# Attention and mixture-of-experts on one Trainium2 core: where the row transposes of the expert blocks stand, and a new placement of the attention part's steps

## What is computed

```python
x = x + retention(layernorm(x), ctx, ctx)       # 16 heads, decayed causal scores, no softmax
x = x + linear_fp8(layernorm(x), kernel, bias)  # input and weights rounded to float8_e4m3fn
x = x + attention(layernorm(x), ctx)            # softmax over 512 context tokens, 16 heads of 16
x = x + experts(layernorm(x))                   # 8 experts of width 512, 4 chosen per token

# experts, for each token n and each of its 4 experts e:
gate, up = split(x[n] @ gate_up[e].T + bias[e]) # 512 each
act = (clip(up, -7, 7) + 1) * min(gate, 7) * sigmoid(1.702 * gate)
y[n] += share[n, e] * (act @ down[e].T + down_bias[e])
```

## Time and profile before

| | |
|---|---|
| runs shown, median (lowest to highest of 3) | 1029.71 us (1019.78 to 1035.69) |
| the profiled execution | 1026.56 us |
| its span, first to last instruction | 1024.8 us |
| mean granted TensorE clock over the span | 0.887 of full speed |
| busy: TensorE, VectorE, ScalarE, GpSimd | 814.2, 641.1, 488.8, 281.7 us |
| first part, about | 0 to 615 us |
| listing the tokens, first blocks | 615 to 666 us |
| blocks 2 to 38 and the last scatters | 666 to 1025 us |

### The profile page before, as it was taken

The page is one execution under the profiler, slowest core; times in us unless marked ns, Lnnn a source line. Parts: engine busy times, 40 slices in busy tenths (PEclk is TensorE's granted clock), DMA queues, the critical chain, the costliest instruction groups (busy, mean ns, idle before and its releaser), DMA issues. The chain is left out here.

```text
span 1024.8 us, 18540 instructions
## 1 busy us (share of the span) xinstructions
PE 814.2 (79%) x6353; PEld 508.4 (50%) x6353; DVE 641.1 (63%) x1238; ACT 488.8 (48%) x950; POOL 281.7 (27%) x261
## 2 busy tenths in 40 slices
PE   0682676778858898887877988999899998999893
PEld 0342232333424343422322354778787887878782
DVE  4546566876687779677788328455555555555552
ACT  1210301455424654366577521466666666666662
POOL 5004003010211000000000002265556555655543
PEclk9895777679868999898696997899999999999997
DMA  7421461016111531034434113133333333333332
GB/s 270 123 60 64 132 167 43 32 54 159 66 50 47 159 75 48 23 106 159 139 125 155 33 41 104 34 55 58 59 64 59 56 57 64 61 56 60 59 43 31
DMA packets 72072, 83.22 MB, mean 81 GB/s; under 512 B 10288, under 2 KB 65200, under 8 KB 71856
## 3 DMA queue, kind: packets, MB, share of 16 engines
q1 hardware_dynamic: 57008, 61.25, 19.5%
q0 software_dynamic: 14976, 20.78, 12.7%
HBM read 52.71 MB, written 29.29 MB: 80 GB/s over the span
## 5 line engine op out<-in xcount | busy, mean ns | idle before, releaser
L1600 PE MATMUL gu_ps<-xt,w 128*128 128x256 f16 x1872 | 215.8, 276 | 29.1 <-ACT xt L1321 29.1
L1600 PEld LDWEIGHTS gu_ps<-xt,w 128*128 (+1 forms) x1872 | 181.7, 99 | 62.9 <-issue 39.5
L672 ACT ACTIVATE p<-st 128x512 f32<-128x512 f32 x256 | 138.7, 595 | 125.2 <-PE st L1156 124.8
L883 DVE TENSOR_REDUCE neg_max<-sc 128x2 f32<-128x1024 f32 x128 | 156.3, 1221 | 59.7 <-PE sc L1132 58.9
L1391 POOL DMA_INDIRECT out<-y,block_rows x78 | 125.1, 1604 | 139.7 <-ACT y L1351 118.6
L1614 PE MATMUL dn_ps<-w,h 128*128 (+1 forms) x936 | 108.6, 273 | 1.4 <-DVE h L1518 1.4
L1509 DVE TENSOR_SCALAR up<-up 128x512 f32<-128x512 f32 x78 | 42.6, 546 | 96.8 <-ACT up L1337 96.8
L1383 POOL DMA_INDIRECT gx<-xr_d,block_rows x78 | 86.0, 1102 | 53.1 <-DVE block_rows L1491 30.1
L1132 PE MATMUL sc<-kz,sq 48*128 48x512 f16 x256 | 63.2, 462 | 42.4 <-DVE neg_max L883 38.7
L1614 PEld LDWEIGHTS dn_ps<-w,h 128*128 128x128 f16 x936 | 89.9, 98 | 11.4 <-issue 1.6
L580 POOL COPY rden_rows<-rden 128x512 f32<-128x512 f32 x16 | 10.8, 677 | 266.8 <-DVE rden L904 266.8
(11 more groups left out here) (200 smaller groups left out, 1114.4 us busy)
## 6 DMA issues: line engine op xcount, KB each, us to landing
stack_d<-t SPq DMA_DIRECT2D x16, 256.0 KB, 2.6
raw<-in_gate_up_t SPq DMA_DIRECT2D x4, 1024.0 KB, 5.0
raw_next<-in_gate_up_t SPq DMA_DIRECT2D x4, 1024.0 KB, 5.6
sq<-stack_d SPq DMA_DIRECT2D x16, 192.0 KB, 3.6
kz<-stack_d SPq DMA_DIRECT2D x16, 192.0 KB, 4.6
sq<-stack_d SPq DMA_DIRECT2D x32, 96.0 KB, 3.2
kz<-stack_d SPq DMA_DIRECT2D x32, 96.0 KB, 3.2
ctx_pad<-in_ctx SPq DMA_DIRECT2D x4, 512.0 KB, 4.0
```

Of the source, the lines that this page charges most:

```text
L672: act.activation(p32[:, n // 2 % RING, 2 * (n % 2) + i, :], st[:, i, :], ACT.Exp, scale=QSCALE).then_inc(s_exp, 1)
L883: dve.tensor_reduce(neg_max[:, qt, :, pair], sc[:], AX.X, ALU.max, negate=True).then_inc(m_max, 1)
L1600: ins = pe.matmul(gu_ps[:, 2 * half + g, q * ROWS:(q + 1) * ROWS], weights(i, wi, slice(col, col + P)), xt[:, i % 2, kd, xi, :], start=(j ...
```

## The change

It has two parts that don't touch each other. In the second part, TensorE issues `turn_x(i+2)` between the two halves of `gate_up(i+1)` instead of behind both; ScalarE issues `take_x(i+2)` ahead of the first `high_half` of block i+1 instead of behind its second `unit`; VectorE issues `collect(i)` ahead of the last `low_half` of block i+1 instead of behind it. In the first part every entry of `ORDER` is new. The steps, their number and what each issues stay, but for the fillers, whose number depends on the order.

```diff
             for i in range(NB):                       # ScalarE
                 if i + 1 < NB:
                     unit(2 * i + 2)
+                    if i + 2 < NB:
+                        take_x(i + 2)
                     high_half(2 * i + 2)
                     unit(2 * i + 3)
-                    if i + 2 < NB:
-                        take_x(i + 2)
                     high_half(2 * i + 3)
                 scale_y(i)
...
                     low_half(2 * i + 2)               # VectorE
                     take_share(i + 1)
                     unit(2 * i + 3)
+                collect(i)
+                if i + 1 < NB:
                     low_half(2 * i + 3)
-                collect(i)
...
-            def gate_up(i):                           # TensorE
+            def gate_up(i, half):
                 pe.wait_ge(xt_ok, i + 1)
-                for half in range(2):
-                    n = 2 * i + half
+                n = 2 * i + half
...
             for i in range(NB):
                 if i + 1 < NB:
                     look_up(i + 1)
-                    gate_up(i + 1)
+                    gate_up(i + 1, 0)
                 if i + 2 < NB:
                     turn_x(i + 2)
+                if i + 1 < NB:
+                    gate_up(i + 1, 1)
                 down(i)
```

Of `ORDER`, the entries that matter below (one tuple per batch):

```diff
-     "quantise": ((84, 89, 93), (250, 256, 263), (504, 505, 506), (777, 785, 793)),
+     "quantise": ((83, 85, 93), (217, 235, 250), (514, 523, 531), (833, 835, 842)),
-     "turn_q": ((97, 99), (271, 287), (511, 516), (812, 827)),
+     "turn_q": ((96, 100), (263, 268), (551, 566), (848, 862)),
-     "max_turn": ((205, 251, 326, 393), (503, 558, 644, 745), (808, 870, 929, 989), (1052, 1112, 1173, 1240)),
+     "max_turn": ((206, 267, 323, 394), (485, 559, 626, 716), (800, 868, 927, 990), (1051, 1109, 1186, 1242)),
-     "turn4": ((739, 746), (950, 965), (1252, 1254), (1313, 1314)),
+     "turn4": ((660, 727), (937, 985), (1168, 1180), (1313, 1314)),
-     "route": ((757,), (974,), (1262,), (1317,)),
+     "route": ((732,), (993,), (1193,), (1317,)),
-     "qk_store": ((39, 41, 128, 150), (175, 177, 353, 388), (489, 493, 646, 675), (805, 809, 925, 967)),
+     "qk_store": ((37, 41, 128, 150), (174, 176, 346, 360), (495, 497, 669, 684), (817, 818, 953, 974)),
```

More of the change, by code:

```diff
@@ L1588, in turn_x @@
                 ins.then_inc(x_tr, 1)
-            def gate_up(i):
+            def gate_up(i, half):
                 pe.wait_ge(xt_ok, i + 1)
-                for half in range(2):
-                    n = 2 * i + half
[L1594 to L1603, removed]
+                n = 2 * i + half
+                for g, (mm, ok) in enumerate(((gate_mm, glu_ok), (up_mm, up_ok))):
+                    need(pe, ok, n - 1)
+                    for q in range(2):
+                        for kd in range(KD):
+                            col = kd * 2 * I + g * I + (2 * half + q) * P
+                            for j, (wi, xi) in enumerate(WX):
+                                ins = pe.matmul(gu_ps[:, 2 * half + g, q * ROWS:(q + 1) * ROWS], weights(i, wi, slice(col, col + P)),
+                                                xt[:, i % 2, kd, xi, :], start=(j == 0 and kd == 0),
+                                                stop=(j == 2 and kd == KD - 1))
+                    ins.then_inc(mm, 1)
             def down(i):
@@ L1653, in _ @@
             list_expert(3)
-            gate_up(0)
+            gate_up(0, 0)
+            gate_up(0, 1)
             for e in range(4, E):
@@ L1682 @@
[L1682 to L1695, removed]
@@ L1709 @@
[L1709 to L1715, removed]
@@ L1763 @@
-     "max_turn": ((205, 251, 326, 393), (503, 558, 644, 745), (808, 870, 929, 989), (1052, 1112, 1173, 1240)),
-     "score": ((218, 222, 226, 236, 241, 253, 257, 261, 276, 283, 289, 296, 304, 311, 316, 319, 361, 372, 380, 387,
[6 rows of a table removed]
-     "values": ((237, 242, 258, 264, 298, 306, 317, 327, 381, 395, 405, 433, 443, 474, 475, 486), (549, 569, 590, 605,
-        634, 640, 658, 688, 703, 751, 753, 761, 774, 782, 790, 799), (851, 863, 883, 898, 912, 937, 943, 956, 984,
-        991, 1003, 1014, 1028, 1040, 1054, 1065), (1099, 1106, 1120, 1139, 1154, 1167, 1182, 1194, 1214, 1227, 1242,
-        1251, 1276, 1286, 1291, 1296)),
@@ L1775 @@
[L1775 to L1779 removed]
+     "turn0_store": ((10, 16, 28, 32), (94, 99, 132, 144), (232, 249, 350, 377), (541, 561, 636, 658)),
@@ new lines @@
+     "stack0": ((36, 52), (142, 168), (369, 412), (653, 740)),
+     "qk_store": ((37, 41, 128, 150), (174, 176, 346, 360), (495, 497, 669, 684), (817, 818, 953, 974)),
+     "next_ctx": ((76,), (200,), (462,)),
+     "stack1": ((138, 147, 159, 165), (363, 381, 428, 487), (707, 713, 719, 801), (967, 979, 1005, 1054)),
+     "next_ctx_t": ((39,), (153,), (507,)),
+     "next_x": ((116,), (309,), (590,), (901,)),
+     "max_store": ((210, 271, 336, 397), (493, 565, 640, 722), (810, 872, 931, 995), (1061, 1114, 1191, 1248)),
@@ new lines @@
+     "x_back": ((124,), (698,), (959,), (1214,)),
+     "out_store": ((662,), (939,), (1166,), (1312,)),
+     "w_load": ((1011, 1013, 1079, 1087, 1125, 1157, 1226, 1253),),
+     "share_store": ((765,), (1031,), (1215,)),
+     "rotate_k": ((3,), (84,), (215,), (489,)),
+     "root": ((1, 81, 113), (115, 209, 303), (312, 502, 593), (599, 809, 908)),
+     "den_spread": ((279, 375, 443, 506), (585, 682, 758, 821), (881, 966, 1023, 1070), (1163, 1218, 1272, 1300)),
+     "root_a": ((632,), (917,), (1135,), (1308,)),
@@ new lines @@
+     "turn0_high": ((7, 14, 24, 27), (89, 95, 130, 137), (229, 238, 347, 364), (516, 552, 627, 642)),
+     "normalise": ((2, 82, 114), (118, 213, 307), (315, 505, 598), (604, 812, 911)),
+     "state_low": ((11, 25), (91, 107), (262, 330), (550, 573)),
+     "qk_high": ((33, 38, 126, 135), (141, 160, 333, 352), (367, 388, 655, 673), (709, 723, 947, 960)),
+     "r_take": ((50, 57, 71, 77), (167, 178, 192, 201), (411, 425, 445, 467), (726, 743, 777, 792)),
+     "v_take": ((18, 22), (55, 59), (499, 508), (814, 822)),
@@ new lines @@
+     "linear_scale": ((105, 109), (276, 287), (575, 588), (878, 894)),
+     "turn3_take": ((120, 122), (318, 324), (633, 645), (921, 926)),
+     "exp": ((220, 222, 225, 239, 242, 248, 254, 257, 290, 295, 301, 308, 319, 328, 334, 341, 355, 372, 380, 391, 402,
[6 rows of a table added]
+     "o_take": ((264, 362, 437, 494), (556, 664, 748, 807), (874, 955, 1014, 1065), (1149, 1211, 1268, 1297)),
+     "normalise_a": ((648,), (918,), (1144,), (1309,)),
+     "rows_high": ((652,), (929,), (1154,), (1310,)),
+     "turn4_take": ((671, 730), (942, 988), (1174, 1184), (1315, 1316)),
@@ new lines @@
+     "w_high": ((1050, 1058, 1062, 1073, 1076, 1078, 1095, 1101, 1108, 1126, 1132, 1139, 1164, 1167, 1176, 1194, 1202,
+        1208, 1252, 1258, 1262, 1277, 1278, 1284),),
+     "route_exp": ((751,), (1019,), (1206,)),
+     "stats": ((0, 80, 111), (112, 207, 297), (305, 484, 591), (592, 804, 903)),
+     "turn0_low": ((8, 15, 26, 30), (90, 97, 131, 140), (230, 244, 348, 366), (536, 558, 631, 646)),
+     "state_sum": ((9, 20), (88, 104), (258, 322), (543, 570)),
+     "rotate": ((4,), (121,), (327,), (606,)),
@@ new lines @@
+     "o_norm": ((288, 393, 454, 586), (612, 691, 763, 828), (886, 981, 1034, 1080), (1185, 1229, 1281, 1302)),
+     "x_bias": ((134,), (721,), (989,), (1250,)),
+     "o_add": ((603, 618), (857, 871), (1093, 1099), (1305, 1306)),
+     "stats_a": ((625,), (909,), (1128,), (1307,)),
+     "rows_low": ((656,), (933,), (1162,), (1311,)),
+     "route_take": ((738,), (1001,), (1199,), (1318,)),
+     "w_low": ((1056, 1063, 1074, 1084, 1085, 1086, 1107, 1113, 1120, 1137, 1145, 1151, 1171, 1190, 1223, 1235, 1241,
+        1247, 1257, 1261, 1266, 1279, 1283, 1288),),
@@ new lines @@
+     "choose": ((739,), (1007,), (1201,)),
+     "weigh": ((761,), (1028,), (1209,)),
+     "turn0": ((6, 12, 21, 23), (87, 92, 125, 133), (226, 233, 338, 351), (510, 547, 622, 637)),
+     "state": ((5, 17), (86, 101), (227, 316), (504, 563)),
+     "r_scores": ((42, 44, 46, 49, 60, 64, 67, 70), (155, 157, 161, 166, 184, 186, 188, 191), (398, 403, 407, 410,
+        424, 432, 438, 444), (680, 686, 692, 725, 762, 769, 773, 776)),
+     "qk": ((29, 34, 123, 129), (139, 149, 329, 345), (361, 385, 649, 670), (685, 718, 930, 954)),
@@ new lines @@
+     "r_outs": ((47, 54, 68, 74), (163, 172, 189, 196), (408, 416, 441, 459), (720, 736, 774, 783)),
+     "r_back": ((58, 61, 73, 78), (170, 180, 194, 203), (414, 430, 448, 471), (729, 745, 781, 796)),
+     "v": ((13, 19), (51, 56), (491, 501), (806, 815)),
+     "turn_q": ((96, 100), (263, 268), (551, 566), (848, 862)),
+     "linear": ((103, 108), (273, 284), (574, 584), (875, 891)),
+     "turn3": ((117, 119), (310, 320), (629, 641), (915, 922)),
+     "maxima": ((145, 148, 152, 171, 177, 181, 195, 199, 211, 214, 218, 231, 236, 245, 251, 259, 272, 277, 283, 289,
[6 rows of a table added]
@@ new lines @@
```

(6 more changed lines are left out.)

63 lines of the change are left out of this document (14 added, 49 removed), and 48 rows, old and new, of the table ORDER.

## The result

The changed kernel takes 990.93 us (median of 4 runs, 983.78 to 991.85); the kernel before, beside it, 1029.24 us (4 runs). The ratio is 0.9642, with a 95% interval of 0.9557 to 0.9727: faster, by 38 us. The forecast was 982, with a range of 968 to 1003. The sign, the range and the expert part came true; the first part didn't give what the sum took for it, and one reason given for the expert part was not the cause, as the experiments show.

What follows compares the result with a forecast made beforehand. The prediction took a ScalarE and VectorE dependency loop to bound the expert blocks. Expert part -37.3 and first part -10.3 took the profiled 1026.56 us to 979.0, forecast as a 982 us median, range 968 to 1003.

Steps and rivals of the forecast that it cites:

- The ring: Expert blocks: a dependency loop through ScalarE and VectorE, `glu` to `glu`, sets 9.13 us a block and shrinks to 8.15.
- Rival 1: Expert blocks: ScalarE and VectorE stay the bound at 8.4 or 8.5 us a block, total 989 us; chance 0.16.
- rival 3: Expert blocks: transposes in mid-block wait themselves, some 9.1 us a block, total 1014 us; chance 0.04.
- The 0.92 that goes: Expert blocks: TensorE's 0.92 us idle before each block's gate matmuls goes, as moved transposes ready `xt` some 3 us early.
- 8.25 us a block: Expert blocks: TensorE becomes the bound at 8.25 us, from 9.247 on average, saving 35.9 us over 36 blocks.
- The first two blocks and the end: Expert part's edges: first two blocks, at low clock, gain about nothing; the last `y_raw` comes 1.4 us earlier.
- TensorE's table loads: Expert blocks: loads of 0.54 to 1.48 us hide behind the previous `down`, cost 0; without cover, 6 us.
- The fillers: First part's tail: filler matmuls fall from 113 to 84, taking 6.3 us off the path.
- The rest of the order: First part, steps in new places: -4 us for one long wait, 0 for everything else, ends +15 and -8.
- 8.27-us wait: First part: TensorE's idle before 294.25 during batch 1's quantising on VectorE; between -8.3 and 0 us, taken as -4.
- rival 2: First part: the new order brings 0 to +9 us while the expert part gives -37.3, total 992 to 1001; chance 0.20.
- rival 4: First part: more idle lowers TensorE's mean clock; from about 0.73 it eats the whole gain, at 0.70 1043 us; chance 0.04.

Runs made afterwards that it cites:

- e9: Kernel before with only VectorE's `collect` moved ahead of the last `low_half`, transposes left behind both halves: 991.93 us, ratio 0.9646.
- e4: Kernel before, old order, with transposes between the halves and `take_x` early, but `collect` left behind the last `low_half`: 1030.62 us, one run.
- e3: Kernel before with the three expert-block edits, old order, no fillers ahead of `turn4` of batches 0 to 2: 983.92 us, ratio 0.9568.
- e7: Same kernel as e3, run again on another chip (expert-block edits, old order, `turn4` fillers only for the last batch): 986.24 us, ratio 0.9613.
- e2: Kernel before with only the new order, old expert blocks: 1022.96 us, ratio 0.9952.
- e5: The whole change against the kernel before, run again on another chip: 988.47 us, ratio 0.962.
- e6: Kernel before with the three expert-block edits and the old order, same kernel as e1 run again: 989.72 us, ratio 0.9636.
- e8: Same as e7 but without the fillers behind the score steps of the first part's tail: 979.35 us, ratio 0.9531.
- e1: Kernel before with the three expert-block edits and the old order: 985.66 us, ratio 0.9581.

## Why the prediction was right, and where not

**The ring.** Right, and shown from both sides. `y_raw` behind the low half was what closed the ring of 9.13 us; with `collect` alone moved the block is 8.31 (e9), with everything but `collect` moved it is 9.13 (e4). One reading of the rows was loose: it says that each step starts within 0.05 us of the end of the one it needs, while the second `glu`, `y_raw` and the next `glu` start 0.08 to 0.10 before that end; the sum goes by starts, so nothing hangs on it. Rival 1 (the ring stays the bound at 8.4 or 8.5) and rival 3 (the transposes wait) are out.

**The 0.92 that goes.** The prediction said that "`xt` of the next block is ready some 3 us before it is wanted and the 0.92 goes", as the effect of the transposes' new place. The slack of 3 us came (3.6), but it isn't what removed the wait: e9 has the transposes in their old place and no wait. TensorE's idle 0.92 was the shadow of the ring. So the step that failed in the expert part is this one, a cause given to the wrong edit; the sum didn't suffer, since all three edits came together.

**8.25 us a block.** Mis-sized by 0.06. The prediction took 9.13 - 0.92 = 8.21 and added 0.04 for one more switch between groups. e9 has no such switch and takes 8.31 as well. Its 48 gate and up loads take 5.23 us; in the kernel before, behind the gap, they took 5.13. So behind a gap TensorE's block is 0.1 us shorter (e4's 24 loads behind a gap of 0.93 take 2.52 too, for 2.61), and only 0.82 of the 0.92 could come back. The loop gives 36 x (9.247 - 8.312) = 33.7 us where 35.9 were forecast.

**The first two blocks and the end.** "Gain about nothing" was wrong for the first two: from the last `turn4` to block 2's first `glu` it is 666.33 - 611.09 = 55.2 before and 666.49 - 613.81 = 52.7 after, so 2.6 us gained. Behind the last first-half `glu` it is 1024.8 - 999.23 = 25.6 and 990.1 - 965.74 = 24.4: 1.2 of the 1.4 forecast. Together 33.7 + 2.6 + 1.2 = 37.4 for a forecast of 37.3: two errors that cancel, not a precise sum.

**TensorE's table loads** cost nothing, as taken: seven of 0.57 to 1.73 us are in the trace, and the mean block (8.312) is the steady one (8.31). The Trainium skill's depth of 64 for TensorE's queue ("TensorE: Matmul & The Clock Gate", its table of specs) agrees with that; no row counts the queue.

**The fillers.** 84 of 113 remained, as counted, and the tail is 6.5 us shorter (forecast 6.3), and 6 to 7 us shorter in the other profiles with 83 or 84 of them. This is right where it is read. In the medians only 1.7 and 3.5 us of it were found (e3, e7), neither clear of the intervals. That TensorE "is not waiting for anything" in that stretch was not so: it waits 2.48 us for `x_rows` ahead of batch 3's `turn4`.

**The rest of the order: the step that failed.** "I take -4" for the 8.27-us wait, and 0 for everything else. The wait is gone from the trace after, and the new order does come to lead; the 0 is what was wrong. The marks give the size, by the means of nine profiles with the old order, which all have the same code up to the last turn of maxima, and four with the new. The new order reaches the last turn of batch 1 17 us earlier (366.0 against 383.1), needs 13 us more from there to the first turn of batch 2 (36.1 against 23.3), and 8 us more from there to the last of all (157.0 to 161.7 against 148.4 to 151.5). Each of the three is outside the spread of the profiles, but their sum is not: the last turn of maxima lies at 550.6 to 560.8, mean 557.0, with the old order, and at 557.1 to 566.0, mean 560.7, with the new. So the rest of the order costs some 3.7 us by these means, in place of -4; that it costs anything isn't clear of the spread, that it gained 4 isn't borne out. With the tail's -6.5 the new order nets about -3. The timed comparisons lie on both sides of that: -5 alone (e2), +5 and -1 beside the expert edits. The first part was to give 10.3, and they put it between 5 gained and 5 lost; that is near rival 2, which had 0.20, on top of a right expert part.

**The clock** (rival 4) didn't turn: the mean granted clock is 0.88 after and 0.887 before. But the first part can be read only as well as it repeats: the same code ahead of the same mark spread over 10 us between profiles of the old order. The profiled execution of the kernel after is one of the late ones: the same kernel reached its last `turn4` at 604.93 in e5 and at 613.81 here. The 2.7 us "lost" between the two profiles shown first are within that spread.

**A version that is better than both**, on the same chip as e5 and e6. Expert edits, the old order, no fillers ahead of batch 2's `turn4` and none at the score steps (e8): 979.35 us, 0.9531 (0.9501 to 0.9562), against 0.962 (0.9588 to 0.9652) for the whole change.

## What to carry to other kernels

Follow the ring before you follow the wait: the engine that idles shows where the time is seen, not where it is made, and a single VectorE step ahead of another gave here all that three edits gave. Count of such a wait only what the engine can take back at its own steady pace. In a hand-written order, a long wait that goes is worth only the lead that is left at the last mark that all versions share, so compare several such marks, over several profiles. And filler matmuls have two sides: on the path they cost their own time (6.5 us of the tail for 30), in waits they held the clock up here (0.91 with them, 0.69 without); take away only those that stand where real work would follow at once.

## What the hardware showed that I had not expected

The clip of the first half took 0.68 us before, under the first scatter on GpSimd, and the prediction put the 0.25 down to that overlap. After the change it takes 0.43 (mean 428 ns over all 78, the group of L1509 above), and it still lies within the scatter: clip 784.50 to 784.93, scatter 783.59 to 785.21. What changed is its place in it, 0.91 us after the scatter's start and not 0.65. So overlap alone doesn't lengthen it. The rule weighed in the prediction (the Trainium skill, "SBUF — State Buffer", "Who interferes with whom": a VectorE operation in a two-port mode and one of GpSimd block each other for a whole instruction) would have made this clip wait for the scatter's end; the trace disagrees. The traces of all 14 kernels say what the place has to do with it. Each of the 158 clips that began 0.58 to 0.89 us after a scatter's start was longer, and ended as if it had been held until 0.9 us after that start (0.85 to 0.92) and had then taken its 0.43. All that began up to 0.47 us after it, or later than 0.90, took 0.43 or 0.44. One from the kernel after, which began 0.89 behind:

```profile
826.02 1.63 POOL L1391 DMA_INDIRECT out<-y,block_rows  x1 [2.85 <-ACT y L1351]
...
826.91 0.45 DVE L1509 TENSOR_SCALAR up<-up 128x512 f32<-128x512 f32 x1 [1.63 <-ACT up L1337]
```

Gathers do it too: the three clips that began 0.67 to 0.74 us after one took 0.50 to 0.57, as if held until 0.81. Nearly all others that lay over a gather began 0.4 us after its start and took 0.43, which is why the prediction saw the lengthening only under scatters. What GpSimd does in that part of the instruction no row shows.

The other is how little the first part repeats. Nine profiles of one and the same code ahead of the last turn of maxima differ by 10 us, about 2% of that stretch, more than the whole effect of placing 1,319 steps anew. The granted clock goes with it: from 0 to 550 us it is 0.85 in the two profiles that reach the mark at 550.6 and 550.9 (e8, e1), and 0.81 to 0.83 in the seven that reach it at 556.4 to 560.8. The earliest, e8, and a late one, e7:

```profile
0.00:550.00 550.00, 394.45 (x2736) 176.01 (x2736) 394.71 (x672) 228.08 (x404) 67.05 (x100) 0.85 0.34 102
```

```profile
0.00:550.00 550.00, 402.96 (x2703) 177.71 (x2704) 386.14 (x665) 219.72 (x391) 68.08 (x100) 0.81 0.34 101
```

That the clock alone makes the spread, and why it differs between executions, is not shown.
